# Projections and attention of a two-layer adaLN kernel as one program per engine, with the first max tiles inside the projections

## The chip, the cores and the metric

One Trainium2 chip (trn2), one NeuronCore, one launch. The metric is the time of the whole program on the device in microseconds (us); the median of three runs is what two kernels are compared by.

## The reference, cut to what matters

Two transformer layers over 2048 tokens of width 512. Only the first layer's attention is touched by the change.

```python
h = layernorm(x) * (1 + ca) + sa            # x: 2048 x 512; sa, ca from silu(c) @ wmod
qkv = h @ W_qkv + b_qkv                      # 16 heads of 32
scores = q @ k.T / sqrt(32)                  # causal: later keys get -10000
ctx = softmax(scores) @ v
x = x + ga * (ctx @ W_out + b_out)
# then: norm, feed forward (2048 wide, Hadamard transform), and a second layer
# with linear attention and a feed forward of 1408
```

## The kernel before

Every engine has an instruction stream of its own, written out by hand with semaphores; there is no scheduler. A `nc.Block()` holds one function for each engine and ends in a barrier of all of them. Where a group of buffers ends (an `ExitStack` named `ctx`), its semaphores are cleared and another barrier follows (L50 to L52). SP issues loads, and POOL issues stores of the projections. All float32 products are made of three matmuls on a high and a low part (`product`, L206).

**Projections (L220 to L535).** Four token blocks of 512 (`NB = 4`). For each block there are 12 items (`PER = 12`): item m of block b has number 12b + m. Items 0 to 3 make q for four groups of four heads, 4 to 7 make k, 8 to 11 make v for 128 tokens each. An item is 12 matmuls 512 wide into one of banks 2 to 5 (L369 to L392). For q and k ScalarE writes the high part (L424), VectorE the low part (L490), and POOL stores both to DRAM (L326, L328), each of two buffers being free again once it is stored. For v VectorE adds the bias into `tokens_a` (L499). `block_order` (L274) puts the items in order; as hooks after items 1, 2, 3 and 5 the norm of the next block is made (statistics, square root, z, then transposes by PE into banks 0 and 1, and the split by ScalarE and VectorE). The vectors of modulation use banks 6 and 7 in items 0 to 19 of the whole (`modulate`), and their weights are loaded by SP in order (L316).

**Attention (L540 to L909).** Query block n = 0 to 15 is (head group g, token block j) = divmod(n, 4). It is made of quads: one quad is one key tile of 128 for four heads, that is four `score` matmuls (L747) into banks 3 to 5 and four exps by ScalarE (L838). Two quads are a step; `context` (L785) of a step is the product of the exps with v into bank 6, and on the diagonal their sum with `ones` into bank 7. Off the diagonal POOL first adds the two quads' exps (`add_pair`, L693), and PE sums those (L776). The exps need the row maxima of the scores beforehand: `max_step` is one tile of 128 queries and up to 512 keys, made by PE (L718) into banks 0 to 2 and reduced by VectorE (L862). Query block n has 16 (j + 1) such tiles. When they are done the maxima are negated (L871), turned by PE (L729), split (L852, L854), stored to DRAM and loaded back as two more rows of `qst` (`rows_of_max`, L648, issued by SP). Tiles and turns stand in one list of 656 slots (L593); 27 of them (`PRELUDE`) come before the first score, and `schedule` (L608) spreads the others over the 160 quads, so that the turn of block n is done 5 quads before that block begins, where its inputs allow it. `load(n)` (L636) brings in q and k of a block in six DMAs.

`kst` and `qst` (7 and 4 buffers) lie where the projections' buffers lay, so that all of attention waits for the end of the projections. Beside this POOL sets `ones` and two rows of each `kst` (L701 to L704), loads a slice of the second feed-forward weight (L679), makes eight butterfly operations on it (L688, L689) and stores it (L691), eight times in all, one in each of the query blocks 0, 1, 2, 4, 5, 6, 8 and 9; in block 0 this stands before the first pair sum. In the second quad of a query block's first step VectorE also finishes the block before (L877).

Of the kernel before, what the change touches and what calls it, by code (L numbers as in the profile page):

```python
# [38 lines left out]
def build_program(nc, a, out):  # L39

    with ExitStack() as whole:
        def sb(ctx, name, shape, dt=F32):
            return ctx.enter_context(nc.sbuf_tensor(name, shape, dt))
# [25 lines left out]
        ident16 = sb(whole, "ident16", [P, P], BF16)  # L69
        mask_keys = sb(whole, "mask_keys", [P, 2 * P], BF16)  # L70
        mask_queries = sb(whole, "mask_queries", [P, 2 * P], BF16)
# [3 lines left out]
        tokens_b = sb(whole, "tokens_b", [P, T * D])  # L75


# [27 lines left out]
        class Norm:  # L105
# [3 lines left out]
            def __init__(self, ctx, tag, src, shift, scale, ht_hi, ht_lo, used=None, zbufs=2):  # L109
# [3 lines left out]
                self.stats = sb(ctx, tag + "stats", [P, TB, 6])  # L113
                self.mv = sb(ctx, tag + "mv", [P, 2, TB, 2])
                self.ve = sb(ctx, tag + "ve", [P, 2, TB])
                self.std = sb(ctx, tag + "std", [P, 2, TB])
                self.rstd = sb(ctx, tag + "rstd", [P, 2, TB])
                self.zbufs = zbufs
                self.z = sb(ctx, tag + "z", [P, zbufs, TB, D])
                self.h = sb(ctx, tag + "h", [P, 2, 512])  # L120
# [99 lines left out]
        with ExitStack() as ctx:  # L220
            x0 = tokens_b[:, :].rearrange("p (t d) -> p t d", t=T)
# [4 lines left out]
            ht_hi = sb(ctx, "ht_hi", [P, KT, 2 * 512], F32R)  # L226
            ht_lo = sb(ctx, "ht_lo", [P, KT, 2 * 512], F32R)
            w_hi = sb(ctx, "qkv_w_hi", [P, 3, KT, D], F32R)
            w_lo = sb(ctx, "qkv_w_lo", [P, 3, KT, D], F32R)
            bias_cols = sb(ctx, "qk_bias", [P, 2 * G])  # L230
            bias_v = sb(ctx, "v_bias", [P, D])
            out_hi = sb(ctx, "qk_out_hi", [P, 2, 512], F32R)
            out_lo = sb(ctx, "qk_out_lo", [P, 2, 512], F32R)
            stage = sb(ctx, "const_stage", [P, 6 * P])
            picks = sb(ctx, "picks", [P, P])
            ccol = sb(ctx, "ccol", [P, 2, KT])
            csilu = sb(ctx, "csilu", [P, 2, KT])
            cwide = sb(ctx, "cwide", [P, 2, KT, 32])
            mod_parts = sb(ctx, "mod_parts", [P, 2, D])
            gate_rows = sb(ctx, "gate_rows", [P, 2, 2, D])  # L240
            gate_sign = sb(ctx, "gate_sign", [P, D])
            gate_size = sb(ctx, "gate_size", [P, D])
# [27 lines left out]
                        used=lambda act, b: act.wait_ge(qkv_done, PER * (b - 1)))  # L270
# [3 lines left out]
            def block_order(b, item, modulate, hooks):  # L274


                for m in range(PER):
# [4 lines left out]
                    if m in hooks and b + 1 < NB:  # L282
                        hooks[m](b + 1)

            with nc.Block() as block:
                @block.sync
                def _(sp):
                    xt = tile_rows(a["L0_attn_x"])

                    def load_mod(i):  # L290
                        l, vec = VECTORS[i]
                        if i >= 2:
                            sp.wait_ge(mod_mm, i - 1)
                        w = a[("L0_wmod", "L1_wmod")[l]][:, vec * D:(vec + 1) * D]
                        sp.dma_start(wmod[i % 2], tile_rows(w)).then_inc(wmod_loaded[i % 2], 16)

                    def load_x(b):
                        rows = slice(TB * b, TB * b + TB)
                        sp.dma_start(x0[:, rows, :], xt[:, rows, :]).then_inc(x_loaded[b], 16)
                    sp.dma_start(ccol[:, 0, :], a["L0_c"]).then_inc(c_loaded, 16)  # L300
                    sp.dma_start(ccol[:, 1, :], a["L1_c"]).then_inc(c_loaded, 16)
                    load_x(0)
                    load_mod(0)
                    load_mod(1)
                    sp.dma_start(stage[:], a["const"][:, 0:6 * P]).then_inc(const_loaded, 16)
                    sp.dma_start(picks[:], a["const"][:, 8 * P:9 * P]).then_inc(picks_loaded, 16)
                    for k in range(KT):
                        sp.dma_start(w_raw[0][:, k, :], tile_rows(a["w_qkv"][0])[:, k, :]).then_inc(w_chunk_loaded[k], 16)
                    sp.dma_start(bias_cols[:], a["qk_bias"]).then_inc(bias_loaded, 16)
                    sp.dma_start(bias_v[:], a["v_bias"].broadcast_to([P, D])).then_inc(bias_loaded, 16)  # L310
                    load_x(1)
                    sp.dma_start(w_raw[1], tile_rows(a["w_qkv"][1])).then_inc(w_loaded[1], 16)
                    sp.dma_start(w_raw[2], tile_rows(a["w_qkv"][2])).then_inc(w_loaded[2], 16)
                    load_x(2)
                    load_x(3)
                    for i in range(2, len(VECTORS)):  # L316
                        load_mod(i)

                @block.gpsimd
                def _(pool):  # L320
                    for e in range(NB * 2 * G):
                        b, m = e // (2 * G), e % (2 * G)
                        hi, lo = ((q_hi, q_lo), (k_hi, k_lo))[m // G]
                        cols = slice(512 * b, 512 * b + 512)
                        pool.wait_ge(qk_hi_ready, e + 1)
                        pool.dma_start(hi[m % G, :, cols], out_hi[:, e % 2, :].bitcast(F32)).then_inc(qk_stored[e % 2], 16)  # L326
                        pool.wait_ge(qk_lo_ready, e + 1)
                        pool.dma_start(lo[m % G, :, cols], out_lo[:, e % 2, :].bitcast(F32)).then_inc(qk_stored[e % 2], 16)  # L328
                    pool.wait_ge(gate_step, 4 * 4)
                    pool.dma_start(gates.rearrange("(one r) d -> one r d", one=1),  # L330
                                   gate_rows[0:1, :, :, :].rearrange("p l g d -> p (l g) d")).then_inc(gates_stored, 16)
                    pool.wait_ge(gates_stored, 16)
                    for i in range(2):
                        pool.wait_ge(qk_stored[i], 32 * NB * G)

                @block.tensor
                def _(pe):
                    def modulate(q):
                        i, second = 2 + q // 2, q % 2
                        (sums if second else products)(i)  # L340

                    def products(i):
                        l, vec = VECTORS[i]
                        pe.wait_ge(wmod_loaded[i % 2], 16 * (i // 2 + 1))
                        if i == 0:
                            pe.wait_ge(cwide_ready, 1)
                        else:
                            pe.wait_ge(mod_copied, i)
                        for k in range(KT):
                            mm = nc.tensor.matmul(bank[6][32 * k:32 * k + 32, :], cwide[:, l, k, :],  # L350
                                                  wmod[i % 2][:, k, :], start=True, stop=True)
                        mm.then_inc(mod_mm, 1)

                    def sums(i):
                        l, vec = VECTORS[i]
                        pe.wait_ge(mod_copied, i + 1)
                        if i == 0:
                            pe.wait_ge(picks_loaded, 16)
                        else:
                            pe.wait_ge(mod_read, i)  # L360
                        if vec in (GA, GB):
                            mm = nc.tensor.matmul(bank[7][:], picks[:], mod_parts[:, i % 2, :], start=True, stop=True)
                        else:
# [39 lines left out]
                def _(act):  # L403
                    def modulate(q):
                        i, second = 2 + q // 2, q % 2
                        if second == 0:
                            copy_parts(i)
# [1403 lines left out]
```

## Time and profile before

| | us |
|---|---|
| runs | 2141.31, 2142.82, 2135.99 |
| median | 2141.31 |
| profiled execution | 2137.04 |
| its span, first to last instruction | 2135.3 |
| PE (TensorE matmuls) busy | 1990.5 (93%) |
| VectorE busy | 1077.6 (50%) |
| ScalarE busy | 638.9 (30%) |
| POOL (GpSimd) busy | 437.0 (20%) |

The mean granted TensorE clock is 0.961 of full speed (1.00 is 2.4 GHz, 0.50 is 1.2 GHz). The duration of a matmul in the timeline contains its way through the array, so matmuls overlap: how long PE needs for one is read from the start of one to the start of the next. In the timeline a bracket is the idle time of that engine before the row and what ended it.

### The profile page before, as it was taken

Reading aid. Unit: us, or ns where it says so; the run is one execution under the profiler, and the core shown is the slowest. Engines: PE = TensorE matmul, PEld = TensorE weight load, DVE = VectorE, ACT = ScalarE, POOL = GpSimd, SP = SyncE. Lnnn points to the kernel's source line nnn. Section 1 sums busy time; section 2 is a strip of 40 time slices with the busy share of each in tenths; the row PEclk is TensorE's granted clock in tenths of the full one; section 3 lists DMA queues with packets and bytes.
Section 4 is the critical chain, followed back from the end, with each engine's and each line's share of the span. In section 5 each row is a group of like instructions: output and inputs, shape, how many; then the busy total and the mean of one; then the engine's idle time right before and its main releaser. Section 6 shows DMA issues by size and latency. Waiting matters only on the chain. (4 is left out here: it accounts for less than half of the span.)

```text
span 2135.3 us, 25645 instructions
## 1 busy us (share of the span) xinstructions
PE 1990.5 (93%) x10088; PEld 1413.0 (66%) x10088; DVE 1077.6 (50%) x1876; ACT 638.9 (30%) x1152; POOL 437.0 (20%) x385
## 2 busy tenths in 40 slices
PE   6997799999999998869999999997998969999998
PEld 4675445554545543758888888886886548888886
DVE  4452677676666641763443434435533574344334
ACT  3221135555555555331112111113221332111111
POOL 0124246767665235400000000000000300000000
PEclk9998599999999999979999999999999989999999
DMA  8625423141221101220000000002001002000002
GB/s 309 213 103 142 87 59 62 32 109 42 67 64 32 31 1 33 96 85 10 30 30 30 30 1 30 0 1 82 10 6 29 2 10 70 20 30 11 15 1 79
DMA packets 61720, 111.86 MB, mean 52 GB/s; under 512 B 6000, under 2 KB 21248, under 8 KB 61568
## 3 DMA queue, kind: packets, MB, share of 16 engines
q1 hardware_dynamic: 54144, 85.05, 14.1%
q0 software_dynamic: 7456, 25.18, 3.9%
q8 instruction: 80, 1.31, 0.3%
q14 instruction: 40, 0.33, 0.1%
HBM read 84.77 MB, written 25.44 MB: 52 GB/s over the span
## 5 line engine op out<-in xcount | busy, mean ns | idle before, releaser
L862 DVE TENSOR_REDUCE part_max<-banks 128x1 f32<-128x512 f32 (+2 forms) x640 | 356.4, 614 | 180.0 <-PE banks L734 113.7
L838 ACT ACTIVATE probs<-banks 128x512 f32<-128x512 f32 (+3 forms) x640 | 310.8, 538 | 338.6 <-PE banks L765 188.1
L734 PE MATMUL banks<-kst,qst 96*128 96x512 f32 (+2 forms) x640 | 274.6, 448 | 24.2 <-DMA kst<-k_hi 13.8
L761 PE MATMUL banks<-qst,kst 98*128 98x512 f32 (+2 forms) x640 | 263.4, 423 | 13.8 <-DMA qst<-max_dram 12.2
L1309 DVE TENSOR_TENSOR tokens_a<-banks,tokens_a 128x512 f32<-128x512 f32 x224 | 151.5, 688 | 72.0 <-PE banks L216 70.3
L761 PEld LDWEIGHTS banks<-qst,kst 98*128 98x128 f32 x640 | 125.2, 196 | 85.7 <-issue 53.2
L214 PE MATMUL banks<-h_hi,f_wg_hi 128*128 128x512 f32 x432 | 170.4, 395 | 12.1 <-DVE f_wg_lo L1273 12.1
L734 PEld LDWEIGHTS banks<-kst,qst 96*128 96x128 f32 x640 | 132.5, 209 | 70.5 <-DVE part_max L862 44.9
L1334 DVE TENSOR_TENSOR tokens_b<-banks,tokens_b 128x512 f32<-128x512 f32 x64 | 44.2, 691 | 267.2 <-ACT tokens_b L1255 267.2
L214 PE MATMUL banks<-f_d_hi,f_hid_hi 128*128 128x512 f32 x432 | 171.0, 396 | 5.9 <-issue 3.6
L215 PE MATMUL banks<-h_lo,f_wg_hi 128*128 128x512 f32 x432 | 169.9, 393 | 0.0
L216 PE MATMUL banks<-h_hi,f_wg_lo 128*128 128x512 f32 x432 | 169.9, 393 | 0.0
L216 PE MATMUL banks<-f_d_hi,f_hid_lo 128*128 128x512 f32 x432 | 169.2, 392 | 0.0
L215 PE MATMUL banks<-f_d_lo,f_hid_hi 128*128 128x512 f32 x432 | 169.1, 391 | 0.0
L214 PE MATMUL banks<-h_hi,f_wu_hi 128*128 128x512 f32 x432 | 168.3, 390 | 0.0
L216 PE MATMUL banks<-h_hi,f_wu_lo 128*128 128x512 f32 x432 | 168.2, 389 | 0.0
L215 PE MATMUL banks<-h_lo,f_wu_hi 128*128 128x512 f32 x432 | 168.1, 389 | 0.0
L1255 ACT ACTIVATE tokens_b<-banks 128x512 f32<-128x512 f32 x64 | 38.3, 598 | 413.4 <-PE banks L216 413.4
L699 POOL TENSOR_TENSOR early_weights<-probs 128x512 f32<-128x512 f32 x96 | 119.8, 1275 | 168.5 <-ACT probs L838 168.5
L798 PE MATMUL banks<-probs,tokens_a 128*32 128x512 f32 (+3 forms) x1280 | 138.4, 552 | 0.0
L699 POOL TENSOR_TENSOR pairs_own<-probs 128x512 f32<-128x512 f32 x96 | 120.0, 1280 | 69.0 <-ACT probs L838 69.0
L1337 DVE SCALAR_TENSOR_TENSOR tokens_b<-banks,f_us,tokens_b 128x512 f32<-128x512 f32 x44 | 33.0, 751 | 185.8 <-ACT tokens_b L1255 171.5
(187 smaller groups left out, 3242.1 us busy)
## 6 DMA issues: line engine op xcount, KB each, us to landing
tokens_a<-in_L_wmod SPq DMA_DIRECT2D x12, 1024.0 KB, 7.0
qst<-q_hi SPq DMA_DIRECT2D x32, 256.0 KB, 6.3
kst<-k_hi SPq DMA_DIRECT2D x32, 256.0 KB, 8.5
tokens_b<-in_L_attn_x SPq DMA_DIRECT2D x4, 1024.0 KB, 12.9
q_hi<-qk_out_hi POOLq DMA_DIRECT2D x16, 256.0 KB, 3.5
q_lo<-qk_out_lo POOLq DMA_DIRECT2D x16, 256.0 KB, 3.7
k_hi<-qk_out_hi POOLq DMA_DIRECT2D x16, 256.0 KB, 3.1
k_lo<-qk_out_lo POOLq DMA_DIRECT2D x16, 256.0 KB, 3.3
```

The source lines that it names most:

```text
L214: nc.tensor.matmul(dst, lh, rh, start=(first and i == 0), stop=False)
L215: nc.tensor.matmul(dst, lh, rl, start=False, stop=False)
L216: mm = nc.tensor.matmul(dst, ll, rh, start=False, stop=(last and i == n - 1))
L699: nc.gpsimd.tensor_tensor(pairs[o % 2][:, h, :], probs[:, 2 * s % PS, h, :], probs[:, (2 * s + 1) % PS, h, :], ALU.add).then_inc(pair_read ...
L734: mm = nc.tensor.matmul(dst[:, 0:wide], qst[0:BIASROW, n % QS, h, P * t:P * t + P], kst[0:BIASROW, (NB * g + c) % KS, h, 0:wide], start=Tr ...
L761: mm = nc.tensor.matmul(dst[:, c0:512], kst[0:BIASROW + 2, ck % KS, h, at:at + P], qst[0:BIASROW + 2, n % QS, h, c0:512], start=True, stop ...
L798: mm = nc.tensor.matmul(bank[6][HD * h:HD * h + HD, c0:512], v[:, kt, at:at + HD], probs[:, q % PS, h, c0:512], start=(kt == 0), stop=(las ...
L838: nc.scalar.activation(probs[:, q % PS, h, c0:512], bank[3 + sh % 3][:, c0:512], ACT.Exp, scale=SCALE).then_inc(exp_done, 1)
L862: nc.vector.tensor_reduce(part_max[:, n % 2, ht, c:c + 1], bank[slot % 3][:, 0:wide], AX_X, ALU.max).then_inc(max_read, 1)
L1255: nc.scalar.activation(silu[:, u % 2, :], bank[2 * (u % 2)][:], ACT.Silu, scale=1.0 if mixed else gs[:, ch:ch + 1]).then_inc(silu_s, 1)
L1309: nc.vector.tensor_tensor(xt, bank[4 + n % 3][:], xt, ALU.add).then_inc(x_added, 1)
L1334: nc.vector.tensor_tensor(act_[:, u % 2, :], up_bank, silu[:, u % 2, :], ALU.mult).then_inc(hid_s, 1)
```

## The change

1. The two blocks and their buffers become one. The functions of the projections are now `qkv_sync`, `qkv_gpsimd` and so on, those of attention `attend_...`, and each engine runs one after the other with no barrier between.
2. The buffers of attention are laid over those of the projections by order of use: the input x has a buffer of its own, q and k of blocks 0 and 1 go where its four blocks were, those of block 2 where z was. `tokens_b` lies at the other end of the memory. What a load overwrites is waited for by itself (`norm.z_ready`, `norm.turned`, `qkv_done`).
3. 49 slots, all tiles of query blocks 0 and 1 and the turn of block 0, move behind the projection items 30 to 46, on banks 6 and 7: 2, 3, 3, 2, 3, 3 behind items 6 to 11 of block 2 and 3 each behind items 0 to 10 of block 3. `PRELUDE` is 49 and nothing stands alone ahead of the first score.
4. POOL sets the two rows of `kst` 0 and 1 before the stores of block 3, the others and `ones` after the projections. SP loads n = 0, 1, 2, then stores the maxima of block 0, then loads n = 3.

```diff
-            with nc.Block() as block:            # projections, then attention in a second block
...
+            def block_order(b, item, modulate, hooks, maxima=None):
...
                     if m in hooks and b + 1 < NB:
                         hooks[m](b + 1)
+                    for slot in (BEFORE[q] if maxima else ()):
+                        maxima(slot)
...
+            mem.close()
+            amem = ExitStack()
+            tokens_b = sb(whole, "tokens_b", [P, T * D], side="right")
...
-            PRELUDE = turn_at[0] + 7
+            PRELUDE = slot_at[(2, 0)]
+            BEFORE = [range(0)] * (2 * PER + 6) + [range(16 * i // 6, 16 * (i + 1) // 6) for i in range(6)] + \
+                     [range(16 + 3 * i, 19 + 3 * i) for i in range(11)] + [range(0)]
...
+            def max_bank(slot):
+                return bank[6 + slot % 2 if slot < PRELUDE else slot % 3]
...
+            def max_tensor(pe, slot):
+                n, i = slots[slot]
+                dst = max_bank(slot)
+                if i == 0:
+                    pe.wait_ge(q_loaded[n % QS], 48 * (n // QS + 1))
+                    pe.wait_ge(k_loaded[n % KS], 48 * (n // KS + 1))
+                if slot == 0:
+                    pe.wait_ge(mod_copied, len(VECTORS))
+                    pe.wait_ge(mod_read, len(VECTORS))
+                elif slot == PRELUDE:
+                    pe.wait_ge(norm.h_ready, KT * NB)
+                    pe.wait_ge(qkv_out, PER * NB - 3)
+                if 2 <= slot < PRELUDE:
+                    pe.wait_ge(max_read, slot - 1)
+                elif slot >= PRELUDE + 3:
+                    pe.wait_ge(max_read, slot - 2)
...
+            def qkv_gpsimd(pool):
+                for e in range(NB * 2 * G):
+                    if e == 3 * 2 * G:
+                        pool.wait_ge(norm.z_ready, TB * NB)
+                        for i in range(2):
+                            nc.gpsimd.memset(kst[i][BIASROW:BIASROW + 2, :, :].bitcast(F32), 1.0).then_inc(ones_ready, 1)
...
+            def attend_sync(sp):
+                def load(n):
+                    if n >= QS:
+                        sp.wait_ge(score_mm, 4 * quads_before(n - QS + 1))
+                    if n < 2:
+                        sp.wait_ge(norm.z_ready, 2 * TB * (n + 1))
+                    elif n == 2:
+                        sp.wait_ge(norm.turned, KT * NB)
+                    elif n == 3:
+                        sp.wait_ge(qkv_done, PER * NB)
+                    if n < NB:
+                        sp.wait_ge(qk_stored[0], 32 * (G * n + 3))
+                    elif n == NB:
+                        for i in range(2):
+                            sp.wait_ge(qk_stored[i], 32 * NB * G)
...
+                for n in range(3):
+                    load(n)
+                rows_of_max(0)
+                load(3)
...
+            def attend_gpsimd(pool):
+                pool.wait_ge(qkv_done, PER * NB)
+                pool.wait_ge(qkv_out, PER * NB)
+                nc.gpsimd.memset(ones[:], 1.0).then_inc(ones_ready, 1)
+                for i in range(2, KS):
+                    nc.gpsimd.memset(kst[i][BIASROW:BIASROW + 2, :, :].bitcast(F32), 1.0).then_inc(ones_ready, 1)
...
             def score(s, half, h):                # in attend_tensor
                 if i == half == h == 0:
                     pe.wait_ge(max_stored[n % QS], 16 * (n // QS + 1))
-                    pe.wait_ge(ones_ready, KS + 1)
+                    pe.wait_ge(ones_ready, n + 1 if n < 2 else KS + 1)
                 if sh >= 3:
                     pe.wait_ge(exp_done, sh - 2)
+                else:
+                    pe.wait_ge(qkv_out, PER * NB - 2 + sh)
...
-                    for slot in range(PRELUDE):   # PE and VectorE, ahead of the first quad
-                        max_step(slot)
...
             with nc.Block() as block:
                 @block.tensor
                 def _(pe):
+                    qkv_tensor(pe)
+                    attend_tensor(pe)
```

## Rows read from the trace of the kernel before

**Rows 1.** Waits of PE, 0 to 420 us: total, times, longest.
```profile
PE banks L734 <- DMA kst<-k_hi: 13.8, 1, 13.8
PE banks L761 <- DMA qst<-max_dram: 12.2, 1, 12.2
```
**Rows 2.** Windows: length, busy time by engine, granted clock, DMA share, GB/s.
```profile
193.50:234.92 41.42, 15.44 (x49) 9.40 (x49) 14.28 (x30) 1.28 (x1) 25.02 (x18) 0.53 0.83 168
234.92:268.96 34.04, 34.04 (x119) 18.71 (x119) 24.94 (x46) 5.88 (x12) 1.16 (x1) 0.52 0.12 30
268.96:292.29 23.33, 21.72 (x114) 11.35 (x111) 19.88 (x38) 8.27 (x16) 4.97 (x4) 0.85 0.32 69
```
**Rows 3.** Timeline of PE, edges of the stretches: start, duration, engine, line.
```profile
193.28 0.39 PE L216 MATMUL banks<-qkv_w_hi,ht_lo 128*128 128x512 f32 x1
...
234.92 0.80 PE L761 MATMUL banks<-qst,kst 98*128 98x512 f32 x1 [12.19 <-DMA qst<-max_dram]
...
258.44 0.41 PE L761 MATMUL banks<-qst,kst 98*128 98x256 f32 x1
...
263.88 3.22 PE L798 MATMUL banks<-probs,tokens_a 128*32 128x512 f32 x16
...
268.96 0.38 PE L761 MATMUL banks<-qst,kst 98*128 98x256 f32 x1
...
277.42 0.86 PE L798 MATMUL banks<-probs,tokens_a 128*32 128x256 f32 x16
```
**Rows 4.** Timeline of VectorE, 16 reduces in a row.
```profile
269.74 8.99 DVE L862 TENSOR_REDUCE part_max<-banks 128x1 f32<-128x512 f32 x16 [5.05 <-PE banks L734]
```
**Rows 5.** Groups by form, VectorE, 300 to 800 us: busy, mean ns, idle before.
```profile
L862 DVE TENSOR_REDUCE part_max<-banks 128x1 f32<-128x512 f32 x375 | 239.7, 680 | 104.9 <-PE banks L734 90.4 <-PE banks L740 12.4
L862 DVE TENSOR_REDUCE part_max<-banks 128x1 f32<-128x256 f32 x102 | 41.9, 415 | 29.0 <-PE banks L740 28.5
L862 DVE TENSOR_REDUCE part_max<-banks 128x1 f32<-128x384 f32 x51 | 27.9, 547 | 6.3 <-PE banks L740 5.9
```
**Rows 6.** Timeline, projection block 3: ends of items 7 (182.62) and 8 (185.34).
```profile
182.62 0.39 PE L214 MATMUL banks<-qkv_w_hi,ht_hi 128*128 128x512 f32 x1
...
183.55 0.75 DVE L490 SCALAR_TENSOR_TENSOR qk_out_lo<-banks,qk_bias,qk_out_hi 128x512 fp32r<-128x512 f32 x1 [1.97 <-ACT qk_out_hi L424]
...
185.34 0.39 PE L214 MATMUL banks<-qkv_w_hi,ht_hi 128*128 128x512 f32 x1
...
185.54 0.69 DVE L499 TENSOR_TENSOR tokens_a<-banks,v_bias 128x512 f32<-128x512 f32 x1 [1.25 <-PE banks L216]
```
**Rows 7.** Timeline of PE: a max tile that waited, and the next instruction.
```profile
322.18 0.50 PE L734 MATMUL banks<-kst,qst 96*128 96x512 f32 x1 [0.39 <-DVE part_max L862]
322.51 0.39 PE L761 MATMUL banks<-qst,kst 98*128 98x512 f32 x1
```
**Rows 8.** Timeline, block 2: low part of item 6, and the start of item 8.
```profile
149.34 0.75 DVE L490 SCALAR_TENSOR_TENSOR qk_out_lo<-banks,qk_bias,qk_out_hi 128x512 fp32r<-128x512 f32 x1
...
149.98 0.39 PE L214 MATMUL banks<-qkv_w_hi,ht_hi 128*128 128x512 f32 x1
```
**Rows 9.** Timeline of POOL: memsets, first butterfly, first pair sums.
```profile
195.55 12.94 POOL L704 MEMSET kst<- 2x2048 f32 x7
...
222.28 1.26 POOL L688 TENSOR_TENSOR tokens_b<-tokens_b 128x512 f32<-128x512 f32 x1 [12.27 <-DMA tokens_b<-in_w2t]
...
280.07 4.97 POOL L699 TENSOR_TENSOR early_weights<-probs 128x512 f32<-128x512 f32 x4 [41.08 <-ACT probs L838]
```
**Rows 10.** DMA issues: KB each, median us from issue to landing.
```profile
tokens_b<-in_w2t POOLq DMA_DIRECT2D x8, 512.0 KB, 7.1
```
**Rows 11.** Windows of 4 us, columns as in rows 2.
```profile
284.00:288.00 4.00, 3.31 (x10) 2.25 (x10) 3.88 (x9) 1.56 (x3) 1.04 (x1) 0.61 0.00 0
...
880.00:884.00 4.00, 2.29 (x13) 1.95 (x14) 3.66 (x4) 1.92 (x3) 2.47 (x2) 0.78 0.00 0
...
1712.00:1716.00 4.00, 2.79 (x12) 2.12 (x13) 4.00 (x7) 0.00 (x0) 0.00 (x0) 1.00 0.00 0
```

More of the change, by code:

```diff
@@ new lines, in attend_scalar @@
+            def attend_scalar(act):
+                for s, (n, i) in enumerate(steps):
+                    for half in range(2):
+                        q = 2 * s + half
+                        c0 = P * max(2 * i + half - TB * (n % NB), 0)
+                        for h in range(4):
+                            sh = 4 * q + h
+                            act.wait_ge(score_mm, sh + 1)
+                            if q >= PS and h == 0:
+                                act.wait_ge(probs_read, q - PS + 1)
+                            if q >= PS and off_diagonal(s - 2):
+                                act.wait_ge(pair_ready, 4 * off_index(s - 2) + h + 1)
+                            nc.scalar.activation(probs[:, q % PS, h, c0:512], bank[3 + sh % 3][:, c0:512],
+                                                 ACT.Exp, scale=SCALE).then_inc(exp_done, 1)
@@ L659, in _ @@
[L659 to L667 removed]
+                    qkv_sync(sp)
@@ L769, in phase @@
-                    def phase(s, half):
-                        tiles = max_of_quad[2 * s + half]
-                        for h in range(4):
-                            score(s, half, h)
-                            for slot in tiles[len(tiles) * h // 4:len(tiles) * (h + 1) // 4]:
-                                max_step(slot)
-                    def sum_pair(s):
-                        n, i = steps[s]
-                        o = off_index(s)
-                        pe.wait_ge(pair_ready, 4 * (o + 1))
-                        for h in range(4):
-                            mm = nc.tensor.matmul(bank[7][HD * h:HD * h + HD, :], ones[:], pairs[o % 2][:, h, :],
-                                                  start=(i == 0), stop=False)
-                        mm.then_inc(pairs_used, 1)
@@ L897, in _ @@
-                    for slot in range(PRELUDE):
-                        max_step(slot)
-                    for s, (n, i) in enumerate(steps):
-                        for slot in max_of_quad[2 * s]:
-                            max_step(slot)
-                        tiles = max_of_quad[2 * s + 1]
-                        for part in range(4):
-                            if n and i == 0:
-                                finalize(n - 1, part)
-                            for slot in tiles[len(tiles) * part // 4:len(tiles) * (part + 1) // 4]:
-                                max_step(slot)
@@ L908, in _ @@
-                    for part in range(4):
-                        finalize(NQ - 1, part)
+                    qkv_vector(dve)
+                    attend_vector(dve)
+            amem.close()
+            both.close()
         def project_out(ctx, tag, there, next_w, bias, src, src_ready, res_ready):
```

986 lines of the change are left out of this document (495 added, 491 removed).

## The prediction

> **What bounds it now.** I read the waits of PE first, because the program is a long row of matmuls and PE works nearly everywhere: what the change can win is where PE stands still or runs slowly. Up to 420 us the largest single waits are two at one place: 13.8 us for the loads of kst and 12.2 us for the rows of maxima of query block 0 [rows 1]. Then the stretches by engine [rows 2]. From the end of the projections to the first score there are 41.42 us, in which PE is busy 15.44; the next 34.04 us have a PE that looks fully busy, but at a granted clock of 0.52, the 1.2 GHz level; the third stretch, 23.33 us, is at 0.85. The edges come from the timeline [rows 3]: the last projection matmul starts at 193.28 and gives way 0.23 us later (193.50), the first score starts at 234.92, the context of step 0 at 263.88, the fourth quad (a quad is four scores and their share of max tiles) at 268.96, the context of step 1 at 277.42. Where max tiles are dense, VectorE sets the pace: 16 reduces back to back in 8.99 us, 0.56 each [rows 4]; alone one takes 0.68, 0.55 or 0.42 by its width [rows 5].
>
> The max tiles before the fourth quad are late because nothing of attention may begin before the block's end; the projections themselves are bound by PE, one item (12 matmuls) per 2.72 us, with VectorE and ScalarE mostly idle beside it [rows 6].
>
> **What goes.** The whole gap of 41.4 us: the barrier, the wait for kst and qst (now loaded in blocks 1 and 2, under matmuls), the 27 max tiles that stood alone, and the trip of the maxima through DRAM, now issued in projection block 3 with some nine items behind it. The schedule, worked out from the goals in the code, was 27, 9, 8, 8, 8, 8, 8 tiles in quads 0 to 6 and becomes 8, 8, 8, 8, 8, 7, 7; from quad 7 on the two are the same. So 22 tiles more leave attention.
>
> Quads 0 to 2 with their context took 34.0 us. New: VectorE first adds the last v tile (done 0.9 us after the end of the matmuls, 0.20 + 0.69 in rows 6), then 24 reduces at 0.56 = 13.5, and I allow 0.7 us, a little over one reduce, for the turn: 15.1. PE runs three banks ahead of it (1.6), so the context starts at 13.5 and takes half of the 5.08 us it took at half clock (263.88 to 268.96 in rows 3), 2.5: 16.0 us. That wins 18.0. The next 23.3 us lose two tiles, 2 x 0.56 = 1.1. **Together 41.4 + 18.0 + 1.1 = 60.5 us.** This supposes that PE, now coming straight from dense work, stays at 2.4 GHz: quads 3 and 4 held it for 9 us (the 8.46 us from 268.96 to 277.42) at the same density.
>
> **What comes.** 49 slots (16 tiles, the turn, 32 tiles) inside projection items 30 to 46, on banks 6 and 7. Two banks: slots a and a+1 go at once, slot a+2 waits for the reduce of slot a, and that reduce stands on VectorE behind the item's own output. Priced from the end T of an item's matmuls. For q and k: ScalarE's high part comes first, VectorE's low part starts at T + 0.93 and takes 0.75, so it ends at T + 1.68 (182.62 and 183.55 in rows 6). Then the reduce: 0.52 as mean of a diagonal row (0.42, 0.42, 0.55, 0.68), 0.60 where every second tile is full. Then the third tile, 0.33 from start to the next instruction after such a wait [rows 7]. An item with three tiles costs 1.68 + 0.60 + 0.33 = 2.61 us, though its tiles are only 1.0 us of PE. For v the output ends at T + 0.89 (185.34, 185.54): 1.82, or 1.74 in block 2. Two tiles never wait: 0.66.
>
> Block 2, items 6 to 11 with 2, 3, 3, 2, 3, 3 tiles: 0.66 + 2.53 + 1.74 + 0.66 + 1.74 + 1.74 = 9.1. The first is special: VectorE is late there from the norm's split (low part at 149.34, when PE is about to end the next item, 149.98) [rows 8], but two banks cover it. Block 3: 8 x 2.61 + 3 x 1.82 = 26.4. **Sum 35.5 us.** Its bounds: below, PE's own 49 x 0.33 = 16; above, the clock (rival 1). I take 35.5, since order on VectorE leaves it no freedom.
>
> **Moved, at no cost.** SP's queue is in order. The load for n=0 stands behind the last modulation load, which goes out in block 1; the one for n=1 waits for the norm of block 3 (about 140 us), two and a half blocks' items before its first tile; the one for n=2 for the turned tiles of block 3. Six DMAs of 256 KB each; if this cover fails, PE stops inside a projection with what is left of a load that took 13.8 us to come in [rows 1]. The load for n=3 waits for the last projection and needs to be there only in quad 6, some 30 us on; rows_of_max(1) is queued behind it, and is wanted about 22 us on. ScalarE waits for the stores of q and k two items back; items get longer, stores don't. POOL is where slack is used up: its memsets, the load of w2, eight butterflies and a store ran in the gap, and it then idled 41.08 us before the first pair sum [rows 9]. New, counted from the end of the projections: five of the seven memsets (1.85 each) about 10, w2 landed at its median of 7.1 [rows 10] 17, butterflies (8 x 1.26) 27, store and next issue about 33, first pair sum (4.97) 38. The first exps that need it come with quad 8, at 16.0 + 22.2 + 4 = 42. Covered by 4 us.
>
> **Sum.** -60.5 + 35.5 = -25.0 us. The profiled execution took 2137.0 us (span 2135.3 and 1.7 around it), which becomes 2112; it lies 4.3 us under the median, so on the median's scale 2141.3 - 25.0 = 2116.
>
> **Rivals.**
>
> 1. *The clock falls a few times* (0.16). Each item now holds a wait of about 1.6 us. For: PE waited for VectorE in quads 5 and 6 and the granted clock fell, 0.61 from 284 to 288 with PE busy 3.31 of 4 us; it fell likewise to 0.78 at 880 among dense 128-row products. Against: at 1712 to 1716 PE was busy only 2.79 of 4 us, in the same kind of products, and the clock stayed 1.00 [rows 11]. Once low, scores and max tiles did not raise it (0.52 in rows 2), the context before 268.96 did. Price: quad 2 took 5.4 us (258.44 to 263.88), so three such and a context at half speed are 21.3 for 16.0, +5.3; an item at half speed is +2.72, three of them +8.2: about 2130.
>
> 2. *The clock stays low through the overlap, the slower end* (0.06). Same place, decided by how many of the 17 items run at 1.2 GHz: all 17 are +46, with quads 0 to 2 +51, so 2116 + 51 = 2167. From (25 + 6.4) / 2.72, about 12 items on, it is slower. Against: at half speed an item is 5.4 us without a pause, and it took the 5.1 us of the context of step 0 to bring the clock back. The Trainium skill's page "TensorE: Matmul & The Clock Gate", section "A second HAM failure mode: psum-queue depth-cycling", speaks for it: PE that pauses briefly between groups because it cycles through PSUM banks oscillates between its two clock levels. By that rule the sum would be this rival's or the one above; the row at 1712 disagrees, the one at 880 agrees.
>
> 3. *The tiles hide better* (0.12): VectorE's reduces slip ahead and the third tile waits little. Then the overlap nears 16 us, for the whole 2097; halfway, 2106.
>
> 4. *POOL is late* (0.06): if w2 takes the 13.5 us that it took here (12.27 of waiting and 1.2 of issue, rows 9), the pair sum is ready at 45 and exps wait some 3 us once: 2119. The same if the loads are late by as much inside the projections.
>
> Forecast as summed: 0.60. What it replaces is so long that only a doubling of the overlap would undo it.
>
> **Range.** From 2103 (rival 3 past halfway) to 2131 (rival 1). A measurement of this kernel can tell about 0.3%, 6.4 us. Faster by more takes the forecast, rivals 3 and 4 and most of rival 1: 0.89; within 0.3%: 0.05; slower: 0.06.
>
> **What would show it.** Right: no wait of PE for kst or for max_dram; the first score follows the last projection matmul within 1 us, at about 229 us; PE waits for part_max inside the projections some 15 times, 1.6 us each for q and k and about 0.8 for v; quad 7 starts near 267 (292.29 now); from there the traces are the same. Wrong: clock windows under 1 between 150 and 229; PE waiting for qst or kst in the projections; ScalarE waiting for POOL after 267.

## The result, and the profile after

| | before | after |
|---|---|---|
| median of 14 runs, us | 2137.07 (2135.34 to 2142.82) | 2127.98 (2125.35 to 2136.40) |
| profiled execution, us | 2137.04 | 2125.41 |
| its span, us | 2135.3 | 2123.3 |
| mean granted clock | 0.961 | 0.974 |

The ratio is 0.9957 (95% interval 0.9948 to 0.9967): 9.1 us faster, where 25.0 were forecast. The two profiled executions differ by 11.6 us, and the steps below are held against that pair. The three runs of before that the prediction had lay high: their median of 2141.31 lies 4.2 us above that of the fourteen, so the forecast of 2116 is a gain of 25.0 on a scale that starts too high.

The waits of PE over the first 420 us of the changed kernel (engine and line, what it waited for, total, times, longest) answer to [rows 1]:

```profile
PE banks L413 <- DVE part_max L441: 22.6, 21, 1.9
PE banks L519 <- DMA tokens_a<-in_L_wmod: 14.1, 2, 9.6
...
PE banks L531 <- ACT mod_parts L582: 2.1, 1, 2.1
```

The waits for kst and for max_dram are gone, as the change says. In their place stand 21 stops of PE for a reduce where before had 5 (2.4 us): 15 of them, 20.2 us, lie among the projections, where before had none. And there is one stop of 2.1 us for mod_parts that the prediction does not have. The stretches answer to [rows 2] (columns as there):

```profile
193.50:244.49 50.99, 39.50 (x141) 29.38 (x141) 19.53 (x33) 4.72 (x6) 5.90 (x11) 0.85 0.14 52
244.49:260.51 16.02, 15.49 (x88) 7.83 (x87) 13.66 (x26) 5.88 (x12) 10.34 (x7) 1.00 0.58 135
260.51:281.20 20.69, 18.89 (x113) 9.81 (x109) 18.52 (x36) 8.16 (x16) 15.54 (x13) 1.00 0.59 125
```

The edges are from the timeline of PE: the first score (244.49), the fourth quad (260.51), quad 7 (281.20).

```profile
244.49 0.39 PE L826 MATMUL banks<-qst,kst 98*128 98x512 f32 x1
```

The three rows carry the whole result. The first score starts **later** than before, 244.49 against 234.92. Quads 0 to 2 then take 16.02 us instead of 34.04, and the next stretch 20.69 instead of 23.33, so that quad 7 starts 11.1 us earlier than in [rows 2] (292.29). After that the two kernels run alike but for a fall of the clock here and there, and the end is 12.0 us earlier.

So the loss is all ahead of the first score. The tiles begin among the projections at 149 us, and the first row holds the later part of the overlap: a clock of 0.85 and a PE busy 39.5 of 51 us. In windows of 4 us (same columns) three places inside projection block 3 look so:

```profile
176.00:180.00 4.00, 2.50 (x8) 2.05 (x9) 2.32 (x4) 0.00 (x0) 1.08 (x2) 0.82 0.36 131
...
184.00:188.00 4.00, 3.53 (x10) 2.80 (x11) 1.57 (x4) 0.00 (x0) 0.54 (x1) 0.67 0.37 135
...
212.00:216.00 4.00, 4.00 (x12) 3.20 (x11) 0.88 (x2) 0.00 (x0) 0.00 (x0) 0.59 0.19 68
```

The timeline of PE shows what an item is there (start, duration, line; the bracket is the idle time before the row and what ended it):

```profile
172.09 0.47 PE L208 MATMUL banks<-ht_hi,qkv_w_hi 128*128 128x512 f32 x1
...
174.93 0.51 PE L413 MATMUL banks<-kst,qst 96*128 96x512 f32 x2
...
177.50 0.51 PE L413 MATMUL banks<-kst,qst 96*128 96x512 f32 x1 [1.93 <-DVE part_max L441]
177.84 0.40 PE L208 MATMUL banks<-ht_hi,qkv_w_hi 128*128 128x512 f32 x1
...
182.18 0.28 PE L413 MATMUL banks<-kst,qst 96*128 96x256 f32 x1
```

The first item's twelve products take 2.84 us (172.09 to 174.93); two tiles go at once, the third waits 1.93 us; from the first tile to the next item are 2.91 us. That next item's products need 4.34 us (177.84 to 182.18): it is the item in which the clock is down. VectorE over the same stretch shows why the third tile is late:

```profile
175.85 0.75 DVE L659 SCALAR_TENSOR_TENSOR qk_out_lo<-banks,qk_bias,qk_out_hi 128x512 fp32r<-128x512 f32 x1 [2.63 <-ACT qk_out_hi L593]
176.75 1.02 DVE L441 TENSOR_REDUCE part_max<-banks 128x1 f32<-128x512 f32 x2
178.04 0.69 DVE L441 TENSOR_REDUCE part_max<-banks 128x1 f32<-128x512 f32 x1 [0.27 <-PE banks L413]
```

VectorE's next instruction is the item's own low part, which waits for ScalarE until 175.85. The two tiles that PE began at 174.93 are made by 175.6, but their reduces stand behind the low part and start at 176.75, and the third tile waits for the first of them.

The missing time can be laid out from these rows. The first score was forecast at 229.0 and came at 244.49, 15.5 us late. 2.1 of it is the stop for mod_parts. Seven items of block 3 have their products at 4.12 to 4.42 us, 30.3 in all, where seven at 2.85 are 19.95: 10.4. What is left, 3.0, is in the size of the items: 2.85 for the products of most, not 2.72, and 2.57 to 3.11 (2.81 in the mean) for three tiles behind a q or k item of block 3, not 2.61; the tiles in block 2 took 8.3, not 9.1, and give some of it back. Whether these three are causes, and whether the stops themselves could go, is what the experiments ask.

### The profile page after: what moved, and what is told of

Its sections match the earlier page's. It is cut to its first block and busy times, and to the rows that moved or that the text cites. A ratio compares the mean times of both kernels' runs of the same rounds, so it can differ in the third digit from the quotient of the medians.

```text
span 2123.3 us, 25631 instructions
## 1 busy us (share of the span) xinstructions
PE 1982.2 (93%) x10088; PEld 1408.4 (66%) x10088; DVE 1077.6 (51%) x1876; ACT 638.8 (30%) x1152; POOL 439.4 (21%) x385
## 3 DMA queue, kind: packets, MB, share of 16 engines
q8 instruction: 80, 1.31, 0.3%
## 5 line engine op out<-in xcount | busy, mean ns | idle before, releaser
L413 PE MATMUL banks<-kst,qst 96*128 96x512 f32 (+2 forms) x640 | 261.4, 420 | 31.4 <-DVE part_max L441 28.2
L826 PE MATMUL banks<-qst,kst 98*128 98x512 f32 (+2 forms) x640 | 259.1, 416 | 1.6 <-ACT probs L903 1.5
L413 PEld LDWEIGHTS banks<-kst,qst 96*128 96x128 f32 x640 | 122.8, 192 | 80.8 <-DVE part_max L441 68.6
L1534 POOL TENSOR_TENSOR w_lo<-early_weights,w_hi 128x512 fp32r<-128x512 f32 x4 | 5.1, 1318 | 592.7 <-ACT w_hi L1588 592.7
```

The lines of the kernel that those rows point to most:

```text
L413: mm = nc.tensor.matmul(dst[:, 0:wide], qst[n % QS][0:BIASROW, h, P * t:P * t + P], kst[(NB * g + c) % KS][0:BIASROW, h, 0:wide], start=Tr ...
L826: mm = nc.tensor.matmul(dst[:, c0:512], kst[ck % KS][0:BIASROW + 2, h, at:at + P], qst[n % QS][0:BIASROW + 2, h, c0:512], start=True, stop ...
```

## The experiments

Each is the changed kernel with one edit unless it says otherwise. "Before" had medians of 2134.95, 2137.28 and 2136.67 us on the three occasions, and the ratios are to these.

**A third bank.** Theory A says that the bank wait makes both the stops and the low clock. Rival B says that the clock falls because max tiles and loads stand among the products, whether PE stops or not, so that another bank takes the waits away and leaves the clock at 0.6 to 0.9.

```diff
-                return bank[6 + slot % 2 if slot < PRELUDE else slot % 3]
+                return bank[(6, 7, 0)[slot % 3] if slot < PRELUDE else slot % 3]
...
-                if 2 <= slot < PRELUDE:
-                    pe.wait_ge(max_read, slot - 1)
-                elif slot >= PRELUDE + 3:
+                if slot >= 3:
                     pe.wait_ge(max_read, slot - 2)
```

(Bank 0 is the norm's too, so the wait for norm.h_ready moves to slot 0.)

> The changed kernel with the 49 early max tiles on three banks (6, 7, 0) in place of two, their places unchanged, so that no third tile waits for a reduce of its own item. Theory A (the order on VectorE holds the third tile back 1.9 us behind a q or k item and 0.8 us behind a v item, and these stops pull the granted clock down): PE waits for part_max inside the projections fall from about 20 us to under 2, the granted clock is 1.00 there, first score at about 214 us instead of 244.5, whole time about 2098. Rival B (the clock falls because max tiles and loads stand among the products, not because PE stops): waits go, but the clock windows between 176 and 232 us stay at 0.6 to 0.9; about 2109.

Measured: 2092.69 us, ratio 0.9803 (0.9788 to 0.9817), and, run again beside another set, 2094.33, 0.9801 (0.9787 to 0.9814). Below are PE's wait in 144 to 245 us, the window over block 3 and the first score in the timeline:

```profile
PE banks L411 <- DVE part_max L439: 1.1, 3, 0.5
...
176.00:232.00 56.00, 55.28 (x271) 37.48 (x270) 42.10 (x79) 13.60 (x25) 23.40 (x27) 1.00 0.38 110
...
209.81 0.39 PE L824 MATMUL banks<-qst,kst 98*128 98x512 f32 x1
```

The same window and the same wait of the changed kernel:

```profile
176.00:232.00 56.00, 41.21 (x131) 30.40 (x131) 20.77 (x36) 6.09 (x8) 9.15 (x17) 0.79 0.21 76
...
PE banks L413 <- DVE part_max L441: 20.2, 15, 1.9
```

Fifteen stops of 20.2 us in all become three of 1.1, the clock is 1.00 instead of 0.79, and the first score comes 34.7 us earlier, with the same 49 tiles in the same places. B falls; A was right in kind and 5 us too careful (2098 and 214 us were expected). The overlap now costs 209.81 - 193.50 - 2.2 (the stop for mod_parts is still there) = 14.1 us, or 0.29 per tile; the change's costs 244.49 - 193.50 - 2.1 = 48.9.

The same kernel was timed a second time beside three others, for a common scale:

> The same kernel as the one with three banks, run again beside the late load and the larger share inside, so that 2 us can be told: about 2093, ratio to the kernel before 0.980.

**The stop filled.** This keeps the bank wait and its length and gives PE work in it: ahead of the third tile stand 8 products (3 for v) whose result nobody reads. It computes nothing else and leaves nothing out.

```diff
+                    if len(BEFORE[q]) == 3 and slot == BEFORE[q][2]:
...
+                        for _ in range(8 if q % PER < 2 * G else 3):
+                            nc.tensor.matmul(bank[0][:], w_hi[:, 0, 0, 0:P], ht_hi[:, 0, 512 * (q // PER % 2):512 * (q // PER % 2) + 512],
+                                             start=True, stop=True)
+                    max_tensor(pe, slot)
```

> The changed kernel, with products that nobody reads (8 of 128x512 behind each q or k item with three tiles, 3 behind each v item) put into PE's stop before the third tile; the stop itself is as long as before. It adds work of no use and leaves the result alone. Theory A: the clock stays at 1.00 through the projections, items of 4.35 us go back to 2.85 and nothing else changes: first score at about 234, whole time about 2117, some 10.5 us less than the change. Rival B (the stops themselves cost, the clock's fall is beside the point): 2128, no gain.

Measured: 2114.47 us, 0.9912 (0.9889 to 0.9934); first score at 232.67. The timeline of PE and the window:

```profile
174.58 2.09 PE L569 MATMUL banks<-ht_hi,qkv_w_hi 128*128 128x512 f32 x8
176.75 0.50 PE L413 MATMUL banks<-kst,qst 96*128 96x512 f32 x1
177.09 0.40 PE L208 MATMUL banks<-ht_hi,qkv_w_hi 128*128 128x512 f32 x1
...
179.83 0.28 PE L413 MATMUL banks<-kst,qst 96*128 96x256 f32 x1
...
232.67 0.39 PE L836 MATMUL banks<-qst,kst 98*128 98x512 f32 x1
...
176.00:232.00 56.00, 55.49 (x244) 41.22 (x244) 26.16 (x45) 6.10 (x8) 8.76 (x17) 1.00 0.21 76
```

The third tile is no sooner relative to its item, but the next item's products take 2.74 us (177.09 to 179.83) instead of 4.34, and the clock is 1.00. Work that serves nothing makes the kernel faster: by 11.1 us between the two profiled executions (2125.41 and 2114.29). The medians lie 13.5 us apart, but they are of different occasions, and the median of before was itself 2.1 us lower on that of the filled kernel. Of the 11.8 us by which the first score is earlier, 0.9 is a shorter stop for mod_parts (1.2 us); 10.9 is the clock alone, beside the 10.4 counted above. That splits the 48.9 us: 10.9 clock, 23.9 stops (232.67 - 1.2 against 209.81 - 2.2), 14.1 what the tiles cost with a third bank.

**No tiles inside.** The merging of the programs is kept, and the 49 tiles run behind the projections in one row.

```diff
-            BEFORE = [range(0)] * (2 * PER + 6) + [range(16 * i // 6, 16 * (i + 1) // 6) for i in range(6)] + \
-                     [range(16 + 3 * i, 19 + 3 * i) for i in range(11)] + [range(0)]
+            BEFORE = [range(0)] * (NB * PER)
...
+                for slot in range(PRELUDE):
+                    max_tensor(pe, slot)
```

(VectorE has the same loop with its reduces.)

> The changed kernel, one program without the barrier and with the early loads, but all 49 max tiles and the turn after the last projection item instead of between items. Theory A: the 49 tiles go at VectorE's pace, 49 x 0.55 = 27 us, and end at 195.6 + 28 = 224 us, 20 us sooner than now; the clock may fall during them as PE is half idle, which adds up to 7 us to the first quads: 2108 to 2116. Rival C (putting tiles under the projections is what brings the gain, and the barrier's end little): slower than the change, above 2128.

Measured: 2116.90 us, 0.9914 (0.9899 to 0.9928), a little over the expected span. Its PE timeline and two windows:

```profile
193.87 0.28 PE L412 MATMUL banks<-kst,qst 96*128 96x256 f32 x1
...
229.55 0.78 PE L829 MATMUL banks<-qst,kst 98*128 98x512 f32 x1
...
194.00:229.55 35.55, 30.91 (x83) 16.95 (x81) 26.82 (x51) 0.00 (x0) 22.62 (x17) 0.56 0.36 82
...
196.00:250.00 54.00, 50.04 (x149) 27.77 (x152) 40.62 (x75) 5.88 (x12) 21.59 (x16) 0.53 0.26 60
```

Forty-nine tiles alone take 35.7 us (28 were expected, with some loss of clock: it falls to 0.56 over the tiles and is 0.53 over the 54 us that take in the first scores). The same tiles hidden under the projections took 48.9. So as made, the part of the change that was to hide work cost more than doing nothing of the kind: 11.1 us between the medians (2127.98 against 2116.90), about 9 between the two ratios, which allow for the occasion, and 6.3 between the profiled executions (2125.41 and 2119.13). The first score comes 14.9 us earlier here, but quad 7 (273.76) only 7.4, since the scores behind the tiles run at the low clock.

**Maxima first.** On VectorE alone, the reduces of the tiles go ahead of the item's own output instead of behind it; still two banks.

```diff
                 for m in range(PER):
-                    item(b, m)
                     q = PER * b + m
+                    if first:
+                        for slot in BEFORE[q]:
+                            maxima(slot)
+                    item(b, m)
```

> The changed kernel with two banks as it is, but on VectorE the reduces of an item's tiles stand ahead of that item's own output. Theory A: the third tile waits about 0.4 us, the overlap costs 17 x 1.35 = 23 us instead of 49, no fall of the clock: first score at 219, about 2103. If the output of the item then comes too late for PE (bank of item n+4, stores), PE waits for qkv_out instead, visible as waits on qk_out_lo.

Measured: 2100.80 us, 0.9839 (0.9824 to 0.9853); first score at 217.76. The wait of PE, 144 to 220 us, and a window:

```profile
PE banks L416 <- DVE part_max L444: 5.9, 15, 0.6
...
176.00:232.00 56.00, 51.19 (x236) 35.23 (x237) 37.46 (x68) 11.92 (x20) 18.41 (x22) 1.00 0.35 106
```

It waits as often as in the change, 15 times, but 0.6 us at most (5.9 in all, not 20.2): the length of the stop was the item's output standing ahead of the reduce, and stops of 0.6 us leave the clock alone. Item outputs that come too late for PE, the other thing that was thought possible, do not show among its waits.

**Two tiles in each item.** No item holds a third tile; the tiles begin sooner, at item 22.

```diff
+            BEFORE = [range(0)] * 22 + [range(2 * i, 2 * i + 2) for i in range(24)] + [range(48, 49), range(0)]
```

> The changed kernel on its two banks, with never more than two tiles behind an item: the 49 slots stand behind items 22 to 46 (of which items 25 to 29 stand beside the norm of the last block). Theory A (a stop comes only where a third tile waits for a reduce of its own item): as good as three banks, first score at about 210 us, clock 1.00, 2093. Rival D (two banks are too few wherever VectorE is behind): PE waits for part_max in block 2, 5 us and more, about 2100.

Measured: 2102.09 us, 0.9837 (0.9824 to 0.9851), as rival D has it; first score at 217.27. Its waits of PE, 60 to 300 us, a row of the timeline and the window behind it:

```profile
PE banks L412 <- DVE part_max L440: 4.4, 7, 1.7
PE banks L412 <- DMA kst<-k_hi: 2.0, 1, 2.0
...
138.48 0.38 PE L412 MATMUL banks<-kst,qst 96*128 96x256 f32 x1 [1.70 <-DVE part_max L440]
...
140.00:144.00 4.00, 4.00 (x14) 2.82 (x12) 0.58 (x2) 0.13 (x1) 0.54 (x1) 0.57 0.20 72
```

The long stops of block 3 are gone, but stops turn up beside the norm in the middle of block 2, where VectorE is late, and once the load for n=1 has not landed. The row at 138.48 is the only stop for a reduce up to 145 us, and the clock behind it is 0.57: one stop of 1.70 us, with two tiles behind it, was enough here, while that of 1.31 us in block 2 of the change (155.01) left it at 1.00. "Two tiles never wait" holds only where VectorE keeps up.

**The load for n=0 later**, on top of three banks. The store of a low part in block 1 was thought to be held up by the six loads that now run beside it.

```diff
+                    if n == 0:
+                        sp.wait_ge(qkv_done, 20)
```

> Three banks, and the load of query block 0 waits until 20 projection items are done, so that its 1.5 MB no longer run beside the stores of q and k of block 1. If these loads delay the stores (ScalarE waited 7.7 us for a store of q there, PE 2.1 us for ScalarE), both waits go back to what the kernel before had (4.7 and 0) and the first score comes 2 us sooner than with three banks alone: about 2091 against 2093. If the store is late for another reason, no difference.

Measured: 2091.50 us against 2094.33 for three banks beside it; first score 207.29 against 209.64. The stop for mod_parts (1.5 us there, 2.2 in the earlier trace of three banks) is gone. What causes it reads from the changed kernel's rows of ScalarE, PE and SP's queue, and last the row of ScalarE with the later load:

```profile
104.20 0.69 ACT L593 ACTIVATE qk_out_hi<-banks,qk_bias 128x512 fp32r<-128x512 f32 x1 [7.75 <-DMA q_lo<-qk_out_lo]
105.41 1.12 PE L531 MATMUL banks<-mod_parts,picks 128*128 128x512 f32 x2 [2.08 <-ACT mod_parts L582]
...
93.31 0.43 SPq L730 DMA_DIRECT2D qst<-q_hi  x1
...
96.23 0.64 SPq L732 DMA_DIRECT2D kst<-k_hi  x1
...
101.31 0.69 ACT L591 ACTIVATE qk_out_hi<-banks,qk_bias 128x512 fp32r<-128x512 f32 x1 [4.55 <-DMA q_lo<-qk_out_lo]
```

ScalarE stands 7.75 us for a store of q_lo; behind it in its queue is the piece that writes mod_parts, and PE waits for that. With the load moved away the wait is 4.55 (before, 4.67), so the loads made it long. The two medians are 2.8 us apart, and on this occasion no run of one kernel (2089.89 to 2092.60) reaches those of the other (2093.32 to 2095.24); the intervals of the two ratios overlap, 0.9774 to 0.9801 and 0.9787 to 0.9814, and three banks on their first occasion began at 2091.74. The moved stop is shown by the traces. It had lasted 1.5 us; the rest of the 2.8 can lie in the clock, which was 0.88 from 232 to 260 us in the trace of three banks and 1.00 in this one.

**More tiles inside.** PRELUDE is 76 instead of 49: two tiles behind each of items 24 to 31, on banks 6 and 7, and four behind each of items 32 to 46, on banks 6, 7, 0 and 1, with the later load.

```diff
+            PRELUDE = 76
+            BEFORE = [range(0)] * 24 + [range(2 * i, 2 * i + 2) for i in range(8)] + \
+                     [range(16 + 4 * i, 20 + 4 * i) for i in range(15)] + [range(0)]
```

> The late load, and 76 slots in place of 49 inside the projections: two behind each of items 24 to 31 on two banks, four behind each of items 32 to 46 on four banks. 27 tiles fewer stand in quads 0 to 6, where VectorE sets the pace at 0.56 us a tile. If PE pays 0.29 us for a tile in either place: first score at 209.8 - 2 + 27 x 0.29 = 216, the 37 us to quad 7 become about 25, whole time about 2087. If quads 0 to 6 are held by the exps or by the pair sums instead, the first is won back less: 2092.

Measured: 2103.25 us, 0.9844 (0.9830 to 0.9857): a miss by 16 us. The first score is at 222.08, 6 us late, with stops up to 1.8 us beside the norm in block 2, where its first tiles still have two banks. And this, from the timeline of PE and POOL:

```profile
256.36 4.93 POOL L795 TENSOR_TENSOR early_weights<-probs 128x512 f32<-128x512 f32 x4
...
258.40 0.79 PE L834 MATMUL banks<-qst,kst 98*128 98x512 f32 x1 [5.50 <-ACT probs L911]
```

The first pair sum on POOL is ready at 261.3, and the exps that need it are now due before. PE stops 5.5 us, and the clock falls to 0.50 behind it. To test that, the steps at which POOL's later pieces run were each moved on, and nothing else:

```diff
-                mixed_at = {n: s for s, n in enumerate((0, 1, 2, 4, 5, 6, 8, 9))}
+                mixed_at = {n: s for s, n in enumerate((1, 2, 4, 5, 6, 8, 9, 10))}
```

> The kernel with 76 slots inside and nothing else changed but POOL's slices, which start with query block 1. If ScalarE's 7.3 us of waiting for pair sums and PE's 5.5 us for its exps come from POOL's memsets, load and butterflies ahead of the first pair sum, both go and the clock's fall after 256 us with them: about 2095, 8 us less than 2103. If not, the same 2103.

Measured: 2093.79 us, 0.9800 (0.9784 to 0.9817), 9.5 us less, where 8 were expected. The trace has to be read with care, for it is of an execution of 2102.66 us, while the three others took 2092.90 to 2094.42. In it the waits for POOL and the stop of 5.5 us are gone, and the stretch from quad 7 to the last score takes 553.1 us where it took 562.7 with POOL's pieces in the old place. But quad 7 comes 3.3 us later, and 5.6 us are lost behind attention. Why stays open. So the trace shows that the stop went, and the medians what that was worth.

**A version put together from what was learned.** Four banks, four tiles in each of the last 17 items (PRELUDE = 68), none beside the norm of block 2, the load for n=0 later, POOL's pieces moved on.

```diff
+            PRELUDE = 68
+            BEFORE = [range(0)] * 30 + [range(4 * i, 4 * i + 4) for i in range(17)] + [range(0)]
...
+                return bank[(6, 7, 0, 1)[slot % 4] if slot < PRELUDE else slot % 3]
...
+                if 4 <= slot < PRELUDE:
+                    pe.wait_ge(max_read, slot - 3)
```

> The late load, 68 slots inside, four behind each of items 30 to 46 on four banks, and POOL's eight slices of w2 in query blocks 1, 2, 4, 5, 6, 8, 9, 10 in place of 0, 1, 2, 4, 5, 6, 8, 9, so that it has nothing before the first pair sum but its memsets. If what spoiled the 76 slots was the fall of the clock in block 2 and POOL, both are gone: 19 tiles more at 0.29 bring the first score to 207.3 + 5.5 = 213, and quads 0 to 6 with their contexts shrink from 36.7 to about 26: 2086. If VectorE can't take four reduces beside an item, PE waits for part_max inside the projections and the time is above 2091.

Measured: 2085.30 us (2082.72 to 2087.01), 0.9761 (0.9746 to 0.9775), the fastest kernel here, 51 us below before and 43 below the change; 2086 was expected. Waits of PE, 60 to 300 us, and the two edges:

```profile
PE banks L414 <- DVE part_max L442: 1.7, 4, 0.7
...
212.26 0.39 PE L829 MATMUL banks<-qst,kst 98*128 98x512 f32 x1
...
241.15 0.50 PE L829 MATMUL banks<-qst,kst 98*128 98x512 f32 x1
```

The clock is 1.00 from 100 to 270 us. The 19 tiles more make the first score 5.0 us later than with the later load alone (207.29), and quad 7 follows 28.9 us behind it instead of 36.7 in the change (281.20 - 244.49); about 26 were expected.

## Why the prediction failed, step by step

**What bounds it, and what goes: right.** The gap went whole. Quads 0 to 2 with their context took 16.02 us, the number forecast, at a clock of 1.00 as supposed; 18.0 us were won there. The next stretch was forecast at 22.2 and took 20.69: the fall of the clock in quads 5 and 6, which before had and the sum took over, did not come, 1.5 us better than the sum.

**"What comes": this step failed.** "Two banks: slots a and a+1 go at once, slot a+2 waits for the reduce of slot a" was right in its order and near in its sizes. 15 stops were forecast and 15 came; 1.6 us for q and k was 1.65 to 1.93 in block 3 and 1.31 at item 31, 0.8 for v was 0.63 to 0.96. The term was 35.5 us (its parts add to 35.4) and measured 48.9. Most of the difference is that I took the items at full clock beside stops that do not leave the clock full: 10.9 us, shown by filling the same stops. The other 2.5 are sizes (48.9 - 10.9 = 38.0 against 35.5). The sentence "I take 35.5, since order on VectorE leaves it no freedom" put the clock only at the upper bound, though the text itself said of rival 1 that "each item now holds a wait of about 1.6 us".

**Rival 1** named the mechanism and sized it at three items and 8.2 us; seven items were slow. Its other half, quads 0 to 2 at half clock, did not come. Its 2130 on the scale of 2141.3 is 11 us faster than before, and 11.6 came in the profile, 9.1 in the medians: of all the cases this came nearest, with a chance of 0.16. That its number fits so well is luck. Up to quad 7 the 25.0 forecast lost 10.9 to the clock, 2.5 to the sizes and 2.1 to the stop for mod_parts, and got 1.5 back in quads 3 to 6: 11.0, where 11.1 came. Two of these terms the rival does not have, and one that it has did not come. What led the weighing astray is the row at 1712 [rows 11]. It shows one stretch with PE busy 2.79 of 4 us at full clock, and I let it stand against a pause in every item, fifteen times over. I also compared busy shares and not stops. The timeline of before has these at the two places, and the products behind the one at 880 are not the dense rows that the prediction calls them:

```profile
881.38 1.20 PE L172 MATMUL banks<-ident,n_z 128*128 128x128 f32 x8 [2.73 <-DVE n_z L161]
...
1713.21 0.50 PE L1644 MATMUL banks<-z_hi,spread 128*128 128x512 f32 x1 [1.35 <-DVE tokens_b L1665]
```

A stop of 2.73 us had the low clock behind it, a single one of 1.35 us had not; the stops of the change, 1.65 to 1.93 us and seven items with a low clock, lie between the two. Neither row could settle it, and 0.16 was too little for what they left open.

The Trainium skill's page "TensorE: Matmul & The Clock Gate", section "A second HAM failure mode: psum-queue depth-cycling", says that a PE which pauses between groups because it cycles through PSUM banks oscillates between its clock levels. The changed kernel agrees with it, by 0.79 over 56 us with two banks and 1.00 with three. With two banks and the reduces first it was 1.00 too: it is the length of the pause that counts here, not the number of banks.

**Rival 2**, low throughout, did not come: 7 items of 17, not 12, and 0.88 over the whole overlap (149 to 245 us). Its argument against itself, that an item at half speed is long enough to bring the clock back, fits rows in which slow and full items mix.

**Rival 3** holds for the kernel with a third bank (14.1 us, below even the 16 that I gave as PE's least), not for the change.

**"Moved, at no cost": wrong in one place.** "Items get longer, stores don't" is not so for every store: those of q_lo got no longer at the median (3.3 us, before 3.7), but the longest went from 7.2 to 8.9, and those of k_hi went up at the median from 3.1 to 4.2. With the load for n=0 moved it is 4.8, so that the place of this load is not the reason; what is stays open. In block 1 one store of q_lo held ScalarE 7.75 us (before, 4.67 at the same place) until PE stood still for 2.1. Moving the load away takes that stop out. The other loads were covered as supposed: no wait of PE for kst or qst in the change. A first tile of n=1 at item 30 would come too early for it, though, as the kernel with two tiles each shows with a stop of 2.0 us.

**POOL, and rival 4.** The first pair sum was forecast 38 us after the end of the projections and is done at 283.1 in the change, some 39 behind, with nobody waiting. That POOL's slack is used up, as forecast, is shown by the kernel with more tiles inside, where exactly that wait eats what was won.

**What stays open.** The runs of the change spread over 11 us, more than those of before (7.5), and the longest has the lowest mean clock (2136.4 at 0.969, 2125.35 at 0.975); which items are slow in which run was not traced. The barrier's removal alone, with the loads and the trip through DRAM left in the gap, was not tried.

## What to carry to other kernels

When work is slipped under a bound engine, count the PSUM banks against the pieces that go in at once, and count what the consuming engine has ahead of them in its queue; a piece too many turns hidden work into a stop, and here it cost more (48.9 us up to the first score) than the same work done openly (35.7). A stop of TensorE that recurs in each item is to be priced twice, once as its length and once as the clock behind it, and by rows with a stop of the same length, not with the same busy share. One more bank took both away here, and the reduces ahead of the output all but 5.9 us of the stops and the whole loss of clock. And each gain at the front moves the next queue into view: first the stores beside early loads, then POOL.

## What was not expected of the hardware

- Stops of TensorE of 1.65 to 1.93 us, one every 5.7 to 7.4 us among products of 128 rows, brought the granted clock down to a mean of 0.79 over 56 us, and one of 1.70 us alone to 0.57 over the 4 us behind it; 15 stops of 0.6 us at most left it at 1.00, and so did one of 1.31.
- The same stops filled with products that nobody reads left it at 1.00 and made the profiled execution 11.1 us shorter: for the clock it did not matter what the work was for.
- Max tiles of 96 rows, one behind the other after the projections and paced by VectorE, did not hold the clock: with PE shown busy 30.91 of 35.55 us it was granted 0.56. Whether the rows or the pace did it was not tried.
- Loads of 256 KB beside a store of 256 KB were felt far from the median: the median store of q_lo is no longer than before, its longest one is 1.7 us longer, and that one alone stopped ScalarE for 7.75 us and, behind it, PE for 2.1.
